# A four-lane kernel becomes a six-lane kernel: network attention cut into three lanes, layer 1 cut at head 2, new PSUM banks and the exponential read from PSUM

## What is computed

```
# layer 0, for each of 16 sequences
xn = layernorm(x)
s  = gru(xn)
for l in 0, 1:                               # the network
    q, k, v = split(shift(xn_l) @ wqkv[l])   # 8 heads of 64
    q, k = rotate(l2norm(q)), rotate(l2norm(k))
    o = softmax(q k^T + band mask) v         # windows of 64: each token sees its own and the one before
    x_l = x_l + o @ wo[l]
    x_l = x_l + mlp(layernorm(shift(x_l)))
x1 = x + s * silu(x_l)
# layer 1
xn1 = layernorm(x1)
a = softmax over queries (q1 k1^T) v1        # 16 heads, key size 16, value size 64
out = x1 + (a @ wo1) * silu(expert part + bias)
```

## Time and profile before

| | |
|---|---|
| median of 3 runs | 3840.28 us |
| the profiled execution | 3830.7 us, its span 3828.9 us |
| TensorE matmul busy | 3102.7 us, 81% |
| VectorE busy | 2714.3 us, 71% |
| ScalarE busy | 2401.6 us, 63% |
| GpSimd busy | 933.2 us, 24% |
| mean granted TensorE clock | 0.929 |

### The profile page before, as it was taken

How to read it: one execution, slowest core, us unless ns; L and a number is a source line. 1 busy time by engine, 2 the same in 40 slices (tenths; PEclk the granted TensorE clock), 3 DMA queues, 4 the chain that set the end, 5 groups by cost and what they waited for, 6 DMA issues and landing times.

```text
span 3828.9 us, 55334 instructions
## 1 busy us (share of the span) xinstructions
PE 3102.7 (81%) x19984; PEld 1603.7 (42%) x20144; DVE 2714.3 (71%) x4829; ACT 2401.6 (63%) x5082; POOL 933.2 (24%) x685
## 2 busy tenths in 40 slices
PE   4668787888978787887978888897878789797786
PEld 2444443434444443444444344444444344444241
DVE  3476777868687886868687786868778686868432
ACT  2345666766666675766667676666667676666553
POOL 2021322222122322222132222213232221223100
PEclk7779898999999999999999899999989999999997
DMA  2001000010101001010100101010100101010200
GB/s 68 1 4 46 16 30 32 20 53 16 53 16 50 16 22 47 20 49 20 49 20 26 36 20 53 16 53 16 42 20 20 53 19 50 18 49 13 92 26 11
DMA packets 113451, 122.82 MB, mean 32 GB/s; under 512 B 13427, under 2 KB 86685, under 8 KB 113181
## 3 DMA queue, kind: packets, MB, share of 16 engines
q1 hardware_dynamic: 113180, 119.26, 9.7%
HBM read 64.70 MB, written 54.53 MB: 31 GB/s over the span
## 4 chain that ended last, share of the span: by engine, by line
PE 52%; DVE 26%; ACT 11%; issue 6%; POOL 5%; SPq 1%; DMA 0%; DVEq 0%; POOLq 0%; ACTq 0%
PE pb L573 29%; PE o_bank L573 12%; POOL scratch L1390 4%; DVE nmax L1292 4%; PE s L573 4%; PE pb L668 3%; PE pb L699 2%; DVE stat L1216 2%; ACT ex L1022 2%; DVE scratch L1220 2%; DVE scratch L1196 2%; DVE stat L1186 2%; PE pb L723 2%; DVE side L1158 1%; DVE scratch L1230 1%
## 5 line engine op out<-in xcount | busy, mean ns | idle before, releaser
L1022 ACT ACTIVATE ex<-s,nmax 128x512 f32<-128x512 f32 x1024 | 698.3, 686 | 279.7 <-DVE nmax L1292 257.1
L1292 DVE TENSOR_REDUCE nmax<-s 128x1 f32<-128x512 f32 x1024 | 676.2, 680 | 259.8 <-PE s L573 257.1
L573 PE MATMUL o_bank<-ex,vsc 128*64 128x512 f32 x2048 | 528.2, 638 | 84.6 <-POOL vsc L1424 84.2
L1424 POOL TENSOR_TENSOR vsc<-vrow,rinv 128x256 f32<-128x256 f32 x256 | 157.0, 613 | 1724.2 <-DVE rinv L1300 1724.2
L1385 POOL TENSOR_TENSOR scratch<-scratch 128x1024 f32<-128x1024 f32 x128 | 307.1, 2399 | 564.5 <-DVE scratch L1199 538.5
L573 PE MATMUL s<-qs,ks 96*128 96x512 bf16 x1024 | 345.2, 394 | 82.7 <-ACT ex L1022 82.7
L573 PE MATMUL pb<-wqkv,hsh 128*128 128x512 f32 x768 | 379.1, 622 | 33.8 <-DVE hsh L1179 26.1
L573 PE MATMUL pb<-kT,qT 64*64 64x64 f32 (+1 forms) x6144 | 330.8, 257 | 45.1 <-DVE scratch L1220 12.7
L959 ACT ACTIVATE scratch<-scratch 128x512 f32<-128x512 f32 x256 | 160.7, 628 | 321.1 <-DVE scratch L1220 321.0
L668 PE MATMUL pb<-const,scratch 128*128 128x128 f32 x1024 | 165.3, 308 | 242.2 <-POOL scratch L1390 242.2
L573 PEld LDWEIGHTS pb<-kT,qT 64*64 64x64 f32 x6144 | 282.9, 144 | 98.4 <-issue 98.4
(11 more groups left out here) (190 smaller groups left out, 6108.9 us busy)
## 6 DMA issues: line engine op xcount, KB each, us to landing
parts_store<-side SPq DMA_DIRECT2D x64, 384.0 KB, 2.6
qs<-parts_store SPq DMA_DIRECT2D x128, 192.0 KB, 2.7
ks<-parts_store SPq DMA_DIRECT2D x128, 192.0 KB, 3.2
parts_store<-side SPq DMA_DIRECT2D x64, 256.0 KB, 2.9
parts_store<-side SPq DMA_DIRECT2D x64, 128.0 KB, 2.7
xin<-in_L_attn_x SPq DMA_DIRECT2D x16, 256.0 KB, 3.6
out<-o1T SPq DMA_DIRECT2D x16, 256.0 KB, 4.3
wqkv<-in_L_ffn_wqkv SPq DMA_DIRECT2D x1, 1536.0 KB
```

Source lines behind the costliest of these rows:

```text
L573: return pe.matmul(o, l, r, start=start, stop=stop, skip_group_check=True)
L1022: A(ex[:, w % 2, j, :], s_bank[(2 * NT + c) % SIMS][:], ACT.Exp, bias=nmax[:, c % 8:c % 8 + 1], accum_out=rsum[:, w % 2, j:j + 1]).then_in ...
L1292: V.tensor_reduce(nmax[:, c % 8:c % 8 + 1], s_bank[(2 * NT + c) % SIMS][:], X, ALU.max, negate=True).then_inc(GV, 1)
L1424: G.tensor_tensor(vsc[:, w % 2].rearrange("p (m a) d -> p m a d", a=2), vrow[:, m:m + 2, 2 * V1 * p:2 * V1 * (p + 1)].rearrange("p m (a d) ...
```

## The change

- **Lanes.** Six: **p** (the new flow `qkv`: q, k, v, rotation and transposes) runs `qkv1` of sequence i-1, then `qkv0` of sequence i. **q** (`attn`: score, prob, pturn) runs `attn1` of i-1, then `attn0` of i. **r** (`head`: pv, oturn, wo) runs `head1` of i-1, `head0` of i, then `post0` of i. **s** runs `pre` of i, `gru` of i-1, `post1` of i-1. **g** is cut at head `FIRST` = 2: heads 2 to 15 of sequence i-2 and the projection, then values and heads 0 and 1 of i-1. **x** runs in iteration 17. `xn0` gets two buffers. All `ORDER` strings are new, and `step` loads the stacks of heads 6 to 15 in the later iteration.
- **Banks.** A bank e serves q, k, v, tq and tk alone. The scores of the even heads go to a, of the odd heads to b, and their transposes to the same banks; pv, oturn and wo use c. Layer 1 has two banks instead of three.
- **Buffers.** `l_qk` single instead of double; `l_sq` shares its place with `l_c`; `prob`, `probT`, `o_row`, `oT` have places of their own.
- **Steps.** `score` does both parities of a tile in one step, matmuls alternating between the two. VectorE takes both maxima, negated; the subtraction is gone. ScalarE's exponential reads PSUM, in four instructions of 128 columns with the negated maximum as bias. q and k are copied from PSUM, and one square of 1024 columns from SBUF takes the place of two of 512 from PSUM.

```diff
-SIMS = 3
+FIRST = 2
@@ lanes
-        "a": lane("attn0", 0, STEPS["attn0"]) + lane("post0", 0, STEPS["post0"]) + lane("attn1", 0, STEPS["attn1"]),
-        "s": lane("post1", -1, STEPS["post1"]) + lane("keep0", 0, [("x0",)]) + lane("gru", 0, STEPS["gru"])
-        + lane("pre", 1, STEPS["pre"]),
-        "x": lane("expert", -B, STEPS["expert"][:-1]),
+        "p": lane("qkv1", -1, STEPS["qkv1"]) + lane("qkv0", 0, STEPS["qkv0"]),
+        "q": lane("attn1", -1, STEPS["attn1"]) + lane("attn0", 0, STEPS["attn0"]),
+        "r": lane("head1", -1, STEPS["head1"]) + lane("head0", 0, STEPS["head0"]) + lane("post0", 0, STEPS["post0"]),
+        "s": lane("pre", 0, STEPS["pre"]) + lane("gru", -1, STEPS["gru"]) + lane("post1", -1, STEPS["post1"])
+        + lane("keep0", 0, [("x0",)]),
+        "x": lane("expert", -B - 1, STEPS["expert"][:-1]),
@@ TensorE, score
+                    for par in range(2):
+                        mm(banks[par], identb[:], masks[:, 0 if t == 0 else 1, :, :].rearrange("p h n -> p (h n)"), stop=False)
+                    rows, at = [slice(0, DH), slice(DH, 2 * DH)], P * t
                     for r in range(PAIRS):
+                        for w, c, k in ((0, 0, at + WIN), (1, 0, at + WIN), (0, WIN, at)):
+                            q = slice(at + WIN * w, at + WIN * w + WIN)
+                            n = WIN * (1 + w)
+                            for par in range(2):
+                                last = mm(banks[par][WIN * w:WIN * w + WIN, P * r + c:P * r + c + n], qT[rows[par], r, q],
+                                          kT[rows[par], r, k:k + n], start=False)
@@ ScalarE, q and k
-                    A(l_sq[:, INNER * k:INNER * (k + 1)], src, ACT.Square).then_inc(FA, 1)
-                    A(l_qk[t % 2][:, INNER * k:INNER * (k + 1)], src, ACT.Copy).then_inc(FA, 1)
+                    if t and kind == "q":
+                        need(act, f, "dve", b, ("rot", t - 1), "s1")
+                    A(l_qk[:, INNER * k:INNER * (k + 1)], bank_e, ACT.Copy).then_inc(FA, 1)
+                    if k:
+                        if t:
+                            need(act, f, "pool", b, ("rot", t - 1), "add")
+                        A(l_sq, l_qk, ACT.Square).then_inc(FA, 1)
@@ ScalarE, prob
-                    A(prob[s[1] % 2], prob[s[1] % 2], ACT.Exp).then_inc(FA, 1)
+                    for r in range(PAIRS):
+                        last = A(prob[u % 2][:, r, :], sims[:, P * r:P * r + P], ACT.Exp, bias=top[:, r:r + 1])
@@ VectorE, score
-                    V.tensor_reduce(top, sims, X, ALU.max).then_inc(FV, 1)
-                    V.tensor_tensor(prob[u % 2], sims, top.unsqueeze(2).broadcast_to([P, PAIRS, P]), ALU.subtract).then_inc(FV, 1)
+                for par in range(2):
+                    V.tensor_reduce(top, sims, X, ALU.max, negate=True).then_inc(f.sem["dve"], 1)
@@ layer 1
-                    if c >= SIMS:
-                        need(pe, glob, "act", b, ("sim", (c - SIMS) // 4, (c - SIMS) % 4), "e")
+                    if c >= 2:
+                        need(pe, glob, "act", b, ("sim", (c - 2) // 4, (c - 2) % 4), "e")
```

367 lines of the change are left out of this document (181 added, 186 removed).

## The result

The changed kernel takes 3662.4 us (3657.8 to 3663.2), the kernel before 3839.4 us on the same chip: ratio 0.954, 95% interval 0.952 to 0.955. The forecast was 3466 us with a range of 3290 to 3650 us. The direction was right; the size was not, and the time lies just above the range.

A forecast was written before the change was run, and what follows sets the result against it. Lane a's latency chain was taken to bound the kernel, TensorE's work close behind. Start 305, 14 iterations of 200 and end 350 gave a 3455 us span, 3466 us as run time; range 3290 to 3650 us.

The forecast's parts named there:

- The full iteration: One full iteration: 178.5 us of TensorE work plus 21.5 us idle, 200 us, bounds 188 and 212.
- the idle time: TensorE's idle time in a full iteration: from 35.5 us down to 21.5 us.
- the tighter list: TensorE's list, with three network lanes to choose from, takes 5 us more off the idle time of an iteration.
- the lists don't fit, single buffers, bank e: Rival: another loop from single buffers, bank e and ScalarE's list replaces the old one; 208 to 218 us an iteration, chance 0.20.
- The loop of 143 us: What must come round once per iteration: eight tiles at 12.5 us, last score to wo 15, post0 28.
- the price of a tile: Each q, k, v tile in lane p: 11 us from iteration 0 plus 1.5 us for waits, 12.5 us.
- the risk in layer 1's exponentials: Single-buffer waits in the tiles, queued behind layer 1's exponentials on ScalarE: 1.5 us a tile, bounds 0 and 4.1.
- Scores in one step: Score passes alternating between row halves on TensorE: 4 us an iteration gained, bounds nothing and 9.4 us.
- off the path, worth nothing alone: VectorE's subtractions removed: 11.1 us less VectorE work an iteration, no gain alone except 0.7 us of a unit's latency.
- Start: Iterations 0 and 1: iteration 0 ends at 142, iteration 1 at 305 us instead of 472.9, 168 us gained once.
- End: From iteration 16 on: 153 us plus 196 us, together 349 instead of 278 us, 71 us lost.
- two banks for layer 1: Rival: banks held over 6.9 us become the bound and make it slower; 3956 us at 7.1 us hold, chance 0.05.

The follow-up runs named there:

- the 15.8 of the expectations: Expectation for moving the first tile of the second block's projections to the previous iteration's end, against the changed kernel; measured 3719.0 us.
- masks: Changed kernel with the matmul laying the mask into a score bank issued three times: 3769.0 us; with it left out: 3633.1 us.
- both small edits undone: Changed kernel with score passes one parity after the other, and VectorE's subtraction with one SBUF exponential put back: 3868.4 us, ratio 1.008 to before.

## Why the prediction was wrong where it was

**The full iteration, 117 of the 206 us.** The step that failed is the idle time: 35.5 - 12 + 3 - 5 = 21.5 us. I let 12 us go for GpSimd's q and k, and 13 went (242.2 to 37.2 over 16 sequences). I added 3 for layer 1's banks and they took 1.8. But I charged nothing for what else the change makes TensorE wait for: the copy out of bank e, the one bank of q, k, v and their transposes (4.3 us an iteration), and the exponentials whose result the transposes read (4.4), which in the kernel before were through when TensorE came to them. And I took off another 5 for "the tighter list", a choice with no row behind it. With the terms as measured the sum comes out: 35.5 - 13 + 1.8 + 4.3 + 4.4 = 33 us, less 2.7 by which the waits not named here shrank ((68.4 + 70.9 + 29.5 - 125) / 16), 30 us, where 29 came. These are sums over the whole span divided by 16; over the full iterations alone the same rows give -11.2, +1.1, +3.8 and +3.6 on an idle time of 35.2. That is bookkeeping from traces: no run gives bank e a second bank, so what its wait costs in time is not shown. The mechanism of the rival "the lists don't fit, single buffers, bank e" (208 to 218 us, 0.20) is what happened, at its lower end.

**The loop of 143 us** was the reason for thinking the iteration would be bound by TensorE alone, and it was mis-sized. The rows of the changed kernel: the last tile's last transposes, the last residual add after wo, and y in the iteration that starts at 981.47, and below them the first two in iteration 0:

```profile
1127.16 0.60 PE L677 MATMUL e<-const,scratch 128*128 128x128 f32 x4
1148.71 0.28 DVE L1253 TENSOR_TENSOR x<-pb,xn_odd 128x128 f32<-128x128 f32 x1
1172.79 0.75 DVE L1279 SCALAR_TENSOR_TENSOR x<-pb,cols,x 128x512 f32<-128x512 f32 x1 [2.94 <-PE pb L587]
```

```profile
115.09 0.65 PE L677 MATMUL e<-const,scratch 128*128 128x128 f32 x4
130.32 0.29 DVE L1253 TENSOR_TENSOR x<-pb,xn_even 128x128 f32<-128x128 f32 x1 [3.51 <-PE pb L587]
```

Counted to the last transposes, as the forecast counted its 11 us in the earlier trace rows, eight tiles take 146.3 us, 18.3 each (forecast 12.5); the 15.8 of the expectations stops at the eighth tile's sum of squares, at 1108.2. From there to the last wo 21.0 (forecast 15), post0 24.1 (28), and the end stretch 16.8, which I counted in iteration 1 and left out of the loop. That is 208, as it must be, since the pieces fill the iteration. The step that failed here is the price of a tile, 46 us of the loop. I had looked for the risk in layer 1's exponentials, but most of the excess of 5.8 us stands there without them: iteration 0 has no layer 1, and its four tiles take 64.0 us, 16.0 each. There the second tile's q copy waits for the first tile's rotation (1.77 us at 64.82, the single `l_qk`), and the matmuls into bank e wait for the copies out of it; what each costs of the 16 us is not separated. Nor is the loop free of TensorE's own work: TensorE works in 86% of the iteration, so added work shows (masks), while removed work and ScalarE's work don't.

**Where the gain comes from.** I gave it to the lanes; with both small edits undone the lanes, banks and buffers make the kernel 28 us slower. Scores in one step I sized at 4 us; passes of 1.18 us for 24 became 1.15 us for 48, 18.9 - 8 x 1.15 = 9.7 us, all of the upper bound. The Trainium skill, TensorEngine Tiling (Array Packing), Key Properties, says that different tiles multiply in parallel; the trace agrees (48 passes in 1.15 us), and my choice below the middle was wrong. That TensorE's work came out as forecast was luck, two errors met: the matmuls into bank e and the similarities take 95 us more over the span (432.0 against 379.1, and 387.3 against 345.2), 5.9 an iteration. I put it down to their standing alone between two waits. The subtraction I called "off the path, worth nothing alone"; with two score banks it is worth 6.7 us an iteration.

**Start, 50 us.** Iteration 0 takes 106 us (forecast 93): its tiles 64.0 for 50, from there to the last wo 14.6 for 15, post0 27 for 28. Iteration 1 takes 198 (163): its eight tiles 137.6 for 100. It is the mis-sized tile again.

**End, 39.5 us.** The projection of sequence 14 comes 159.6 us after the start of iteration 16 (forecast 133): four tiles 77.9 for 50, to the last wo 20.7 for 15, then 61 for 68. After the experts 13 heads are left, not nine; at 7.9 us each that is 35 us more, of which the stretch before them gives 20 back.

**What held:** no engine's work was off by as much as 5 us an iteration, ScalarE's 9.4 us more cost nothing that shows in the period (7 of them taken out: 208.2), two banks for layer 1 did not become the bound, and the largest wait of before is small now.

**What stays open.** Which of bank e, the single `l_qk` and the order of the lists makes a tile of 16 to 18 us was not tried, nor the lanes without them. How much of the iteration of the kernel before was clock was not tried, nor two score banks in it without the rest.

## What to carry to other kernels

When a change removes the largest wait of an engine, price the idle time by what comes to stand in its place: of 205 us of waiting removed 125 came back, most of it behind a bank that the change had made the only one and behind a step that had been hidden. Small pieces (a subtraction, the order of passes) were worth more here than the scheduling around them, and one that gained 105 us beside a second score bank cost 262 us without it. Measure a piece of the plan to the same mark in both kernels: the tile looked like 15.8 us to one mark and was 18.3 us to the forecast's own. Where TensorE's granted clock falls behind a thin stretch, look at it before you take work away from TensorE.

## What the runs showed of the hardware

- Passes with 64 rows in alternating row halves (and banks) run side by side: 48 in 1.15 us; one half after the other 1.90 us, the pace of an `av` with as many columns (1.94 us).
- Idle time was paid twice here: the clock fell to 0.50 late in a stretch of 6 us in which TensorE worked for 2.5, and the next `av` took 3.68 instead of 1.94 us. Eleven matmuls that nobody reads, 3.5 us in all, kept it at 1.00 there and made the kernel 36 us faster. Leaving 5.2 us of work an iteration out went with a clock of 0.94 instead of 0.96 and gave back 0.9 us an iteration.
